# Where the experts' second bias is added: a product with the choices in the last stage, or a one-row product in the second layer's banks

## The reference, cut to what matters

```python
grouped = x.reshape(b, s // g, g, d)                      # g = 32 tokens in a group, 16 groups per batch item
logits = jnp.einsum('bntd,des->bntes', grouped, Wc) + bc
perm = (logits == jnp.max(logits, axis=-3, keepdims=True))  # each of 32 experts x 4 sets chooses one token per group
permuted = jnp.einsum('bntd,bntes->bnesd', grouped, perm)
inner = jax.nn.relu(jnp.einsum('bnesd,esdf->bnesf', permuted, W1) + b1)     # f = 32
result_permuted = jnp.einsum('bnesf,esdf->bnesd', inner, W2) + b2           # b2: 32 x 4 x 512
result = jnp.einsum('bnesd,bntes->bntd', result_permuted, perm)
```

## Time and profile before

| | us |
|---|---|
| median of three executions | 2254.47 |
| the profiled execution | 2248.99 |
| span of its trace | 2247.2 |
| of this, first stage | to about 1120 |
| experts' stage, of it the two layers' last pass | 1120 to 1428, of it 1240 to 1428 |
| last stage | 1434 to 2247 |

### The profile page before, as it was taken

How to read it: one execution, slowest core, us unless ns; L and a number is a source line. 1 busy time by engine, 2 the same in 40 slices (tenths; PEclk the granted TensorE clock), 3 DMA queues, 4 the chain that set the end, 5 groups by cost and what they waited for, 6 DMA issues and landing times. The chain is left out here.

```text
span 2247.2 us, 39361 instructions
## 1 busy us (share of the span) xinstructions
PE 1885.3 (84%) x14173; PEld 1145.6 (51%) x14211; DVE 1389.0 (62%) x2616; ACT 1251.9 (56%) x2311; POOL 629.1 (28%) x1139
## 2 busy tenths in 40 slices
PE   6999999999999999998577555257789889889875
PEld 3666666666666666665254322015445445445532
DVE  2757767676766757667355444124777777777763
ACT  2666656656655665666155222234776776776753
POOL 1322321322232132231000001004536336336420
PEclk9999999999999999999799766576888989989988
DMA  6433534344353433333187676767525435424200
GB/s 200 133 91 114 153 90 143 83 117 123 114 155 94 143 80 97 101 100 99 68 175 151 188 228 238 283 231 268 174 95 169 144 102 169 157 89 128 67 20 19
DMA packets 215455, 302.86 MB, mean 135 GB/s; under 512 B 62912, under 2 KB 122400, under 8 KB 207968
## 3 DMA queue, kind: packets, MB, share of 16 engines
q1 hardware_dynamic: 156656, 213.79, 30.5%
q10 hardware_dynamic: 42224, 52.97, 7.4%
q0 software_dynamic: 16384, 33.59, 5.8%
HBM read 161.60 MB, written 71.53 MB: 104 GB/s over the span
## 5 line engine op out<-in xcount | busy, mean ns | idle before, releaser
L506 DVE TENSOR_REDUCE a_negmax<-a_score 128x1 f32<-128x512 f32 x512 | 345.3, 683 | 113.1 <-PE a_score L622 105.1
L441 ACT ACTIVATE a_prob<-a_score,a_negmax 128x512 f32<-128x512 f32 x512 | 354.0, 693 | 99.0 <-DVE a_negmax L506 98.2
L317 POOL DMA_DIRECT2D a_q_stack<-a_q_parts x512 | 250.7, 498 | 517.9 <-DVE a_q_parts L500 253.9
L622 PE MATMUL a_score<-a_k_stack,a_q_stack 128*128 128x512 f32 x512 | 354.5, 693 | 10.0 <-ACT a_prob L441 8.3
L630 PEld LDWEIGHTS a_turn<-a_ident,a_prob 128*128 128x128 f32 x2048 | 253.9, 141 | 134.6 <-issue 93.5
L630 PE MATMUL a_turn<-a_ident,a_prob 128*128 128x128 f32 x2048 | 308.8, 274 | 3.4 <-ACT a_perm L417 2.0
L325 DVE COPY a_probT<-a_turn 128x512 f32<-128x512 f32 x256 | 176.2, 688 | 213.5 <-PE a_turn L630 213.3
L325 ACT COPY a_probT<-a_turn 128x512 f32<-128x512 f32 x256 | 150.3, 587 | 280.3 <-PE a_turn L630 278.7
L2001 PE MATMUL c_ff<-c_w2T,c_hqT 128*128 128x512 bf16 x482 | 144.1, 459 | 40.1 <-ACT c_hqT L1537 34.3
L622 PEld LDWEIGHTS a_score<-a_k_stack,a_q_stack 128*128 128x128 f32 x512 | 97.4, 190 | 112.8 <-issue 74.8
L651 PE MATMUL a_mix<-a_probT,a_v 128*32 128x128 f32 x4096 | 138.9, 276 | 0.1
(11 more groups left out here) (210 smaller groups left out, 3335.3 us busy)
## 6 DMA issues: line engine op xcount, KB each, us to landing
a_k_stack<-a_k_parts SPq DMA_DIRECT2D x512, 64.0 KB, 2.6
a_q_stack<-a_q_parts POOLq DMA_DIRECT2D x512, 64.0 KB, 2.3
scratch_res<-b_chosen SPq DMA_DIRECT2D x32, 1024.0 KB, 4.7
c_res<-scratch_res SPq DMA_DIRECT2D x32, 1024.0 KB, 7.6
c_hid<-in_L_ffn_W ACTq DMA_DIRECT2D x16, 1024.0 KB, 7.1
c_negm<-scratch_m SPq DMA_DIRECT2D x64, 256.0 KB, 4.4
a_xs<-in_x ACTq DMA_DIRECT2D x8, 1024.0 KB, 5.4
scratch_cT<-a_cT SPq DMA_DIRECT2D x8, 1024.0 KB, 5.2
```

What stands on the lines that cost most here:

```text
L317: eng.dma_start(stack[kind][i * DH0:(i + 1) * DH0, M % 2, g, :].bitcast(F32), parts[kind][g * DH0:(g + 1) * DH0, part, :].bitcast(F32)).th ...
L441: nc.scalar.activation(prob[:, U % 4, :], score.bank(U)[:, :], ACT.Exp, bias=negmax[:, u:u + 1], accum_out=sums[:, head_of(U), tile_of(U): ...
L506: nc.vector.tensor_reduce(negmax[:, U % UNITS:U % UNITS + 1], score.bank(U)[:, :], AX.X, ALU.max, negate=True).then_inc(max_ready, 1)
L622: nc.tensor.matmul(score.bank(U)[:, :], stack["Q"][:, M % 2, g, t * P:(t + 1) * P], stack["K"][:, M % 2, g, :], start=True, stop=True).the ...
```

## The change

In the experts' stage a tile `ones` of 128 x 128 is filled by POOL. The bias rows of four experts at a time stand in the tile `xn`, which the gather no longer needs by then: set `s` of expert `e` in partition 32 s, 512 wide. SP loads the first four (8 KB each) when the gather's last tokens have been split, and one more after each expert's store. In `second_layer`, PE first multiplies for each set one row of `ones` by the one bias row into the set's bank (`start=True`), and then adds the set's product to it (`start=False`). In the last stage the product with `b2e`, the tile and its load are gone; the last of the four products now tells DVE that the bank is full.

```diff
+        ones = sb("ones", [P, G])
+        bias2 = lambda e: xn[:, e % NB // 2, e % 2 * 2:e % 2 * 2 + 2, :].rearrange("p t w -> p (t w)")
...
+                def load_b2(e):
+                    sp.dma_start(bias2(e)[0:P:F, :], A["L0_ffn_b2"][e]).then_inc(b2_in[e % NB], 16)
...
+                sp.wait_ge(low_ready, PASSES * TILES)
+                for e in range(NB):
+                    load_b2(e)
                 for e in range(EXP):
...
                     sp.dma_start(res_d[e], results(e)).then_inc(res_stored[e % NR], 16)
+                    if e + NB < EXP:
+                        load_b2(e + NB)
...
+                nc.gpsimd.memset(ones[:, :], 1.0).then_inc(ones_set, 1)
...
                     if e % NE == 0:
+                        pe.wait_ge(ones_set, 1)
                         pe.wait_ge(inner_ready, e // NE + 1)
+                        pe.sem_inc(pe_parted, 1)
+                    pe.wait_ge(b2_in[e % NB], (e // NB + 1) * 16)
                     wt.wait_read(pe, 0, e)
...
                     for s in range(SETS):
+                        r = slice(s * F, s * F + 1)
+                        nc.tensor.matmul(work.bank(second_job(e, s))[:, :], ones[r, :], bias2(e)[r, :],
+                                         start=True, stop=False)
+                    for s in range(SETS):
                         j = second_job(e, s)
                         r = slice(s * F, (s + 1) * F)
                         nc.tensor.matmul(work.bank(j)[:, :], inner[r, q % 2, e % NE, :], w2T[r, e % 2, :],
-                                         start=True, stop=True).then_inc(work.full[j % 4], 1)
+                                         start=False, stop=True).then_inc(work.full[j % 4], 1)
...
-        b2e = sb("b2e", [P, D])
...
-                sp.dma_start(b2e[:, :], A["L0_ffn_b2"].rearrange("e s d -> (e s) d")).then_inc(const_in, 16)
...
                     for g in range(GT):
-                        nc.tensor.matmul(bank[g * TG:(g + 1) * TG, :], permT[:, t * P + g * TG:t * P + (g + 1) * TG], res[:, t % 2, g, :],
-                                         start=True, stop=False, skip_group_check=True)
-                    nc.tensor.matmul(bank[:, :], permT[:, t * P:(t + 1) * P], b2e[:, :], start=False, stop=True,
-                                     skip_group_check=True).then_inc(mix.full[j % 2], 1)
+                        last = nc.tensor.matmul(bank[g * TG:(g + 1) * TG, :], permT[:, t * P + g * TG:t * P + (g + 1) * TG], res[:, t % 2, g, :],
+                                                start=True, stop=True, skip_group_check=True)
+                    last.then_inc(mix.full[j % 2], 1)
```

More of the change, by code:

```diff
@@ L759, in experts_phase @@
     GT = P // TG
+    NB = 4
     TILES = B * T
@@ L786, in experts_phase @@
         wt = Ring(ctx, sems, nc, "b_wt", 2, 2)
-        const, zeroed = sem("const"), sem("zeroed")
+        const, zeroed, ones_set = sem("const"), sem("zeroed"), sem("ones_set")
         b1_in, b1_ready = sem("b1_in"), sem("b1_ready")
@@ L794, in experts_phase @@
         w2_sorted = sem("w2_sorted")
+        b2_in = [sem(f"b2_in{k}") for k in range(NB)]
         relu_done, inner_ready = sem("relu_done"), sem("inner_ready")
@@ L1215, in tail_phase @@
             sem(n) for n in ("pe_parted", "pool_parted", "sp_parted", "dve_parted", "act_parted"))
-        N_CONST = 5
+        N_CONST = 4
         head_of = lambda tile, h: tile[:, :, h // 2, (h % 2) * DV:(h % 2 + 1) * DV]
```

## The result

Over 20 executions of each the changed kernel took 2266.67 us (2254.65 to 2273.47) against 2252.86 (2246.18 to 2256.15): the ratio is 1.0061, with a 95% interval of 1.0047 to 1.0075. It is slower by 14 us. I had forecast 2252, no change, with 0.30 on slower; the measured time lies inside the range of 2234 to 2273, but the direction is another than the likeliest case's.

The account below looks back on a forecast made before the run. The prediction took the experts' load loop and, in the last stage, mostly PE as limits; +18 (experts' stage) - 18 (removed products) - 2 (load) = -2 us, put on the median: 2252 us, 8-in-10 range 2234 to 2273.

Parts of the forecast that it names:

- What bounds each stretch: Experts' second pass: a load loop of two experts, 16 loops; last stage, 1600 to 2060 us: mostly PE.
- the other costs there: Experts' stage: bias-row loads on SP, POOL's extra fill and five more semaphores, taken as zero for all.
- The price of the added group: Experts' stage: 17 added groups on the path at 1.1 to 2.05 us each, 19 to 35; 26 us taken.
- 5 us of refunds: Experts' stage: products behind an added group run at 1.14 instead of 2.09 us in about a third of 16 loops.
- my +18: Experts' stage in sum: 26 us for added groups less 5 and 3 us given back; bounds +8 and +35.
- rival 1: Load loop: every added group at 1.2 GHz without refund, +35; last stage gives 15, start 1; +19, 2273 us; chance 0.24.
- The groups of the other experts: Load loop: added groups of experts whose products lie inside the load's wait cost nothing; uncovered, up to 33 us more.
- What is taken away: Last stage: 32 products with `b2e` removed, 18 us gained (bounds 13 and 25.6), plus 2 us for the load.
- an earlier fall of the clock: Last stage: without the removed products the clock falls earlier in some items, taking back a microsecond or two each.
- rival 4: Experts' stage: one-row products take turns instead of running side by side, 71 to 136 us, some 2310 to 2360; chance 0.04.
- (3): Load loop: shorter idle time keeps the clock up through the wait, -5 us for the stage; about -28, 2226; chance 0.08.
- (5): Load loop: bias rows come late, so it waits for SP, a few microseconds in each loop, 2290 us; chance 0.02.

Follow-up runs that it names:

- the train: Kernel before plus 24 groups of one-row, then 24 of 32-row products after the experts' stage; 1.71 us a one-row group, 0.86 a 32-row group; ran once.
- the run with the last stage's part alone: Experts' stage of the kernel before with the last stage of the changed kernel, so no second bias at all: 2239.92 us, 0.9949 of before.
- the run with the load kept: Kernel before without the products with `b2e`, no second bias at all, but `b2e` and its 256 KB load stay: 2244.81 us, 0.9962 of before.
- the thinned products: Kernel before with the last stage's product with `b2e` taking one of its 128 rows (bias then wrong): 2275.97 us, 1.0121 of before.

## Why the prediction was wrong

**What bounds each stretch: right.** The load loop was the limit of the experts' pass and carried the added group of every second expert. From the products of expert 1 to those of expert 31 it was 172.56 us before (1251.60 to 1424.16) and 198.82 after (1250.27 to 1449.09): 15 loops, longer by 1.75 us on average, where a group takes 1.87 (1248.40 to 1250.27, start to start at the low clock). Single loops grew by 0.55 to 3.68, so the agreement holds for the sum and not for each. The rest of the 28.0 us lies ahead of expert 1. Nothing speaks against having put the other costs there at zero: with the loads of the bias rows kept, the pass came down to 174.4 us.

**The price of the added group: the step that failed.** The step was "a group put ahead keeps PE at work while the clock rises", with its 5 us of refunds for the products behind it, and the middle of 1.1 and 2.05 for the group itself, which also supposed a rise. The runs showed the reverse: one-row products did not bring the clock up in 41 us of nothing else (the train), and in the changed kernel all 16 groups behind the wait cost the low clock's 1.87 us, and none of the 16 products behind them ran at 1.14. So my 1.06 us net for each of 17 groups was 1.75. With 32 rows in the same place the pass grows by 13.6 to 19.2 us instead of 28.0: there my +18 would have been about right, though by refunds, since most groups behind the wait kept the low price there too. This was rival 1, which I had at 0.24; its 35 us counted 2.05 where 1.87 was measured, and its loops grew by a little less still. I had weighed the transposes' part in the clock, and not the new product's own.

**The groups of the other experts: right that they are off the path, with a limit.** They cost nothing visible in the load's wait, but the waits before the next burst shrank from 4.5 to 4.08 us and in some later loops to 1.5 and less; there is not much cover left.

**What is taken away: right in place, too large in size.** 25.6 us was the bound, 18 my value, 2 for the load; the runs give 7 to 15 for both. The second scatter of an item was hidden as the chain said. What was late next: PE's waits for ACT's and DVE's results, which I had named. I had also named an earlier fall of the clock. Whether that took a part is not settled: the run with the last stage's part alone has a mean clock of 0.90 in its steady stretch, no lower than the 0.89 before, and there the waits account for the shortfall; the run with the load kept has 0.88. The 27 us of the thinned products don't decide it, since these still take PE's time.

**Slips in the working.** The middle of 19 and 35 is 27, not 26, and rival 4's lower end is nearer 2297 than 2310. Neither changes the forecast's direction.

**The other rivals.** The clock didn't hold through the wait (3): the transposes behind every wait of over a microsecond took 1.11 or 1.12 us. The one-row products ran side by side (4), eight records in 2.09 or 1.14 us. The bias rows were never waited for (5). The 4.5 us lost in the last item's drain were the same instructions at another clock in this execution; whether that explains why the changed kernel's executions spread over 19 us and those of before over 10 is not shown.

## What to carry to other kernels

Work added to an engine that idles is free only where it stands inside the wait: find the instruction that waits, and put the new one ahead of it, not behind. Leave it where it is beside instructions that don't wait: with all the one-row groups moved ahead the pass stayed at 207.3 us, with only the odd experts' it fell to 190.0. When PE's bursts are short and start at the low clock, look at a product's height as well as at its length: here a one-row product took the time of one with 32 rows and left the clock down, and giving it its full row group, with zero weights in the other rows, won back 9 us of a cost of 28. And when a large product is taken out of a busy stage, look for what PE then waits for: here 23 us of freed time made the stage only some 10 us shorter.

## What was not expected of the hardware

Continuous one-row products left TensorE at 1.2 GHz for 41 us; after 32-row products of the same length had begun at 1464.6, it ran at 2.4 GHz from 1468 on. In the experts' pass 31 rows of zero weights beside one of ones, over rows of old tokens, did nearly as much as 32 rows of real data (199.9 and 194.3 us, against 208.7 with one row). Thinning 32 full-height products, two records each, in a busy stage cost 27 us without adding an instruction.
